# Four more units of eight tiles and closer final layers in a graph network's edge pass

## The chip, the cores and the metric

The kernel runs on one core of a Trainium2 chip. Its engines run their own instruction streams and wait for each other by semaphores: PE (matrix products), DVE and ACT (vector and scalar work), POOL (here it issues the indirect gathers), SP (here it issues plain transfers). The metric is the time of one execution on the device in microseconds (us), lower is better.

## The reference

```python
h = x                                        # 6250 nodes x 128; 100000 edges, sorted by dst
e = concat([h[src], h[dst]], axis=1)
a_k = exp(relu(e @ W_att_k + b_att_k))       # k = 1, 2, 3
att_k = segment_sum(a_k, dst)
avg_a = (a1/att1[dst] + a2/att2[dst] + a3/att3[dst]) / 3
m = avg_a * relu(relu(relu(h[src] @ W_msg_1 + b1) @ W_msg_2 + b2) @ W_msg_3 + b3)
h_neigh = segment_sum(m, dst) / max(deg, 1)
y = relu(concat([h, h_neigh], 1) @ W_c1 + b_c1) @ W_c2 + b_c2
out = layernorm(x + y)                       # without scale and bias
```

## The kernel before

**Stages.** First the three message layers run over all nodes and leave a table of message rows in memory (to about 69 us). Then one loop runs over units of edges. A tile is 128 edges, a group two tiles (256 edges, 391 groups), a unit four tiles or, in a long unit, eight. The first 108 groups, whose targets are the 512 busiest nodes, are not gathered: they are counted into a matrix (the count stage, units 0 to 26, four groups in each), and this matrix is multiplied with the message table block by block (the hot stage, units 29 to 77, one block of 128 nodes in each). The other 283 groups are gathered, and the loop over units handles them, in order of their target: `LONG` = 22 long units first, then 98 of four tiles, 120 in all. In ten of the long units (3, 5, ... 21) half of the tiles have no gather: their messages are computed from rows of `x` loaded before ("early" tiles).

**One unit.** POOL gathers a tile's message rows with one indirect DMA (L1428) into a ring of 12 places of four tiles; a long unit takes two places, and a place is free again when PE has summed the unit that held it. PE makes the one-hot products of a unit two ahead (`edge_q`, L1567), DVE adds the logits (L2078, and L2084, which waits for the gathered rows), ACT takes the exponent (L1763), DVE makes the weights (`weights`, L2104 and L2109), PE sums messages and weights into the nodes' window (`add_edges`, L1615, L1621), and DVE adds each group's window to the accumulator (`add_sums`, L2128, one add for each group). The order is written out by hand: at each step of the loop each engine's program names what it does next, and waits hold it there.

**Final layers.** When all edges of a block of nodes are in, its final layers start: 14 pieces, number 0 to 9 of four blocks ("wide"). Piece c starts at unit `final_at[c]`, and its steps follow one in a unit: step 0, PE turns the sums (L959, in `add_edges`); step 1, twelve products (L971) for the three heads, into the same three banks for all pieces; DVE makes the scales (L1113 to L1118); step 2, ACT scales the first head (L1050) into `v_fin`, which there is once, and DVE adds the other two for two of the four blocks (L1133); step 3, DVE does so for the other two; step 4, PE multiplies `x` and adds `v_fin` (L979, L982); step 5, ACT's relu (L1058), PE's second product (L987), DVE adds a bias to `x` (L1179); step 6, DVE adds and takes the moments (L1189 to L1197); step 7, ACT and DVE make the standard deviation ("refine", L1202 to L1212); step 8, ACT normalizes (L1100) and SP stores. `FINAL_EVERY` says how many units lie between the starts of two pieces: three after an even one and three after an odd one, so that piece 0 to 9 start at 81, 84, ... 108. In a unit, a step 1 goes first, then the pieces in order. Four waits tie a piece to the one before it:

```python
# wide_pe, step 1 (L971): all of the piece before is scaled
pe.wait_ge(s_fv[0], all_scaled(c - 1))
# wide_pe, step 4 (L979): the piece before has been added (L1189)
pe.wait_ge(s_fy[0], FINAL_Y * (c - 1) + 1)
# wide_act, step 2 (L1050): v_fin of the piece before has been used (L982)
act.wait_ge(s_fr[0], c)
# wide_act, step 5 (L1058): hidden of the piece before has been used (L987)
act.wait_ge(s_f2[0], c)
```

**The left-edge check.** DVE looks whether an edge lies outside its group's window: four steps (`left`) at units 0, 17, 18, 19, then PE transposes the result (L1705) at step 20 into a bank that the counting uses too, and DVE reduces it (`another_pass`, L2063 and L2067) at the end of step 21. So that the bank is free for it, PE waits before the transpose until DVE has added the counts of group 80 (L1940, in step 21), and the product that uses the bank next (group 84, PE's step 21, L1641) waits for the end of `another_pass`. DVE adds counts and makes their one-hots (L1925) in each of the steps 0 to 27; ACT makes the other side (L1782). SP issues a load of the hot logits behind the check.

Of the kernel before, what the change touches and what calls it, by code (L numbers as in the profile page):

```python
# [32 lines left out]
P = 128  # L33
# [20 lines left out]
HOT_GROUPS = 108  # L54
HOT_WIDTHS = (6, 9, 10, 12)
PAIRS = 4
LONG = 22
KEPT = 4608
RING = 12
TWO, THREE = 2, 3  # L60
# [4 lines left out]
EARLY = 10  # L65
EARLY_FROM, EARLY_EVERY = 3, 2
# [29 lines left out]
def gnn_program(nc, x, x_t, src, dst, w_first, w_rest, b_rows, table, hot_table, near_table, q_table, early_table, ok_table, out,  # L96
                n_edges):
    f32, bf16, i32 = mybir.dt.float32, mybir.dt.bfloat16, mybir.dt.int32
    ALU, ACT, AX = mybir.AluOpType, mybir.ActivationFunctionType, mybir.AxisListType.X
# [11 lines left out]
    n_hot = HOT_GROUPS  # L111
# [8 lines left out]
    def width_of(g):  # L120

        if g < n_hot:
            return HOT_WIDTHS[g // CELL]
        share = min(1.0, (g // CELL + 1) * CELL / n_groups)
        mean = 2 * GROUP * n_nodes / n_edges * share
        return min(WIN, 4 * -(-int(mean + 12 * share + 2 + 3.99) // 4))

    def items_of(g):

        w = width_of(g)  # L130
        most = n_blocks if w * n_blocks <= 512 else -(-n_blocks // TWO)
        return [(a, min(a + most, n_blocks)) for a in range(0, n_blocks, most)]

    def items_to(g):

        return sum(len(items_of(h)) for h in range(g))
# [4 lines left out]
    def counted(step):  # L141

        return range(step * PAIRS, min((step + 1) * PAIRS, n_hot))
# [5 lines left out]
    SPLIT_FROM = min(g for g in range(n_hot) if len(items_of(g)) > 1)  # L149
    assert items_to(SPLIT_FROM) == SPLIT_FROM and SPLIT_FROM % PAIRS == 0  # L150
    HOT_AT = COUNT_STEPS
    hot_end = HOT_AT + n_blocks + 2
    long_from = (n_hot // (2 * pair) + 1) * 2 * pair
    long_end = long_from + (LONG - 1) * 2 * pair
    assert long_end < n_groups and CELL % (2 * pair) == 0
# [4 lines left out]
    early_units = [EARLY_FROM + EARLY_EVERY * k for k in range(EARLY)]  # L160
    assert all(len(first_order[n]) == 2 * pair for n in early_units) and early_units[-1] < LONG
    early_groups = [first_order[n][pair:] for n in early_units]
# [17 lines left out]
    with ctx:  # L180
        def sb(name, shape, dt=f32):
            return ctx.enter_context(nc.sbuf_tensor(name, shape, dt))

        def sem(name):
            return ctx.enter_context(nc.semaphore(name))
# [29 lines left out]
        ident = sb("ident", [P, P])  # L215
# [65 lines left out]
        def hot_comb(t):  # L281

            j = t % HOT_RING
            return combs[j % TWO][:, j // TWO, :]
# [31 lines left out]
        least = sb("least", [P, 1])  # L316
        least_all = sb("least_all", [1, 1])
# [20 lines left out]
        bank = [ctx.enter_context(nc.psum_tensor(f"bank{i}", [P, 512], f32)) for i in range(8)]  # L338
# [12 lines left out]
        early_h, early_x, EARLY_BANK = staged[2], staged[1], 3  # L351
# [343 lines left out]
        Q_BANKS, SUM_BANKS, EXP_BANK, SIDE_BANKS = (1, 3), (0, 2), 4, (5, 6, 7)  # L695
# [2 lines left out]
        assert len(HOT_BANKS) == HOT and (HEADS + 1) * P <= 512  # L698
        assert columns_most + UNIT * PARTS <= 512

        LEFT_STEPS, LEFT_PE, LEFT_END = (0, 17, 18, 19), 20, 21


        assert LEFT_END < HOT_AT - 4 and LEFT_PE * PAIRS < n_hot
        ONES_AT = max(LEFT_END, early_units[-1])
        assert ONES_AT < HOT_AT - 2
        COUNT_BANKS = SIDE_BANKS + (EXP_BANK,)
        FOUR = len(COUNT_BANKS)
        LEFT_FREE = (LEFT_PE + 1) * PAIRS - FOUR + 1
        LEFT_NEXT = (LEFT_PE + 1) * PAIRS  # L710
        assert LEFT_NEXT < SPLIT_FROM
        LEFT_BANK = COUNT_BANKS[LEFT_NEXT % FOUR]
        HOT_ADDED = 3
        BOUND_AT, POWER_AT, OK_AT = 1, 2, 10
        BOUND_STEPS, OK_STEPS = 3, 5
# [10 lines left out]
        rest = n_blocks - sum(sizes) - 1  # L726
        sizes += [rest - rest // 2, rest // 2, 1]
        finals = [(sum(sizes[:c]), nb) for c, nb in enumerate(sizes)]
        FINAL_EVERY, FINAL_STEPS = (3, 3), 8
        LAST, LAST_FROM = len(finals) - 1, 2  # L730
        A, B, C = LAST - 3, LAST - 2, LAST - 1
        assert finals[LAST][1] == 1 and finals[B][1] <= LAST_FROM and finals[C][1] <= LAST_FROM
# [65 lines left out]
        s_left = sem("s_left")  # L798
        s_least = sem("s_least")
# [22 lines left out]
        s_erow = sem("s_erow")  # L822
# [7 lines left out]
        s_cadd = sem("s_cadd")  # L830
# [431 lines left out]
        def edge_pass(first):  # L1262

            order = first_order if first else again_order
            n_units = len(order)
            places = [2 if first and i < LONG else 1 for i in range(n_units)]
            place = [sum(places[:i]) for i in range(n_units)]
# [9 lines left out]
            def groups_to(i):  # L1277

                return sum(len(u) for u in order[:i + 1])
# [4 lines left out]
            def width(i):  # L1284
                return width_of(order[i][0])

            n_long = sum(n > 1 for n in places)
            assert all(n > 1 for n in places[:n_long])

# [17 lines left out]
            def early_turn(i):  # L1307

                return i // EARLY_EVERY if first and i < EARLY_EVERY * (EARLY + 1) else None
# [103 lines left out]
            with Straight(nc) if first else nc.Block() as block:  # L1413
# [127 lines left out]
                def _(pe):  # L1541
# [44 lines left out]
                    def first_early(k):  # L1586

                        pe.wait_ge(s_ecopy, k + 1)
                        pe.matmul(bank[EARLY_BANK][:, 0:COLS], w1, early_x, start=True, stop=True).then_inc(s_e1, 1)

                    def second_early(k):

                        pe.wait_ge(s_eh1, k + 1)
                        pe.matmul(bank[EARLY_BANK][:, 0:COLS], w2, early_h, start=True, stop=True).then_inc(s_e2, 1)
# [33 lines left out]
                    def count_edges(step):  # L1628

                        for g in counted(step):  # L1630
                            pe.wait_ge(s_lo, g // TWO + 1)
                            for j, (begin, end) in enumerate(items_of(g)):
                                item, w = items_to(g) + j, width_of(g)
                                if item >= FOUR:
                                    pe.wait_ge(s_cadd, item - FOUR + 1)
                                if item == LEFT_NEXT:
                                    pe.wait_ge(s_left, len(LEFT_STEPS) + 1)
                                for h in range(TILES):
                                    t = g * TILES + h
                                    pe.wait_ge(s_oh, t + 1)  # L1640
                                    pe.matmul(bank[COUNT_BANKS[item % FOUR]][:, 0:(end - begin) * w],  # L1641
                                              hot_lo[:, t % HOT_RING, :], hot_comb(t)[:, begin * w:end * w],
                                              start=h == 0, stop=h == TILES - 1).then_inc(s_ct, 1)
# [41 lines left out]
                    for i in range(n_steps):  # L1685
                        k = early_turn(i)
                        if i < n_units:
                            add_edges(i)
                        if k is not None and i % EARLY_EVERY == 1 and k < EARLY:
                            second_early(k)  # L1690
                        if first and i < COUNT_STEPS:
                            count_edges(i)
                        if k is not None and i % EARLY_EVERY == 0 and k < EARLY:
                            turn_early(k)
                        if i + 2 < n_units:
                            edge_q(i + 2)
                        if k is not None and i % EARLY_EVERY == 0 and k < EARLY:
                            first_early(k)
                        if k is not None and i % EARLY_EVERY == 1 and k < EARLY:
                            third_early(k)  # L1700
                        if i == LEFT_PE:
                            pe.wait_ge(s_left, len(LEFT_STEPS))
                            if first:
                                pe.wait_ge(s_cadd, LEFT_FREE)
                            pe.transpose(bank[LEFT_BANK][0:1, 0:P], least[:, :], ident[:, :]).then_inc(s_least, 1)  # L1705
                        if first and 0 <= i - HOT_AT - 2 < n_blocks:
                            hot_edges(i - HOT_AT - 2)
                        if first and i == hot_end:
                            turn_hot()
                        for c, step in final_steps(i):  # L1710
                            final_pe(pe, c, step, groups_to(ready[c]))
# [158 lines left out]
                def _(dve):  # L1870
# [189 lines left out]
                    def another_pass():  # L2060

                        dve.wait_ge(s_least, 1)
                        dve.tensor_reduce(least_all[:, :], bank[LEFT_BANK][0:1, 0:P], AX,  # L2063
                                          ALU.min).then_inc(s_left, 1)
                        dve.wait_ge(s_left, len(LEFT_STEPS) + 1)
                        if first:
                            dve.scalar_tensor_tensor(more[:, :], least_all[:, :], DONE, late[:, :],  # L2067
                                                     ALU.is_lt, ALU.max).then_inc(s_left, 1)
                        else:
                            dve.tensor_scalar(more[:, :], least_all[:, :], DONE, None, ALU.is_lt).then_inc(s_left, 1)  # L2070
# [65 lines left out]
                    for i in range(n_steps):  # L2136
# [40 lines left out]
                        if i == LEFT_END:  # L2177
                            another_pass()
# [119 lines left out]
```

## Time and profile before

| | |
|---|---|
| median of 3 runs | 774.49 us (770.85 to 776.41) |
| profiled execution | 772.04 us, of which the span of instructions is 767.9 us |
| mean granted clock of PE | 0.864 of full speed |
| busy: PE, DVE, POOL, ACT | 85%, 77%, 72%, 63% of the span |

A row of the timeline gives the start in us from the start of the span, the length of the row in us, engine, line, operation, names, the number of instructions that it merges, and in brackets the idle time before it with what ended it. Matmuls of 32-bit data stand as two records each.

### The profile page before, as it was taken

The page shows a single profiled execution, that of the slowest core. Times are in us where ns is not written, and L with a number is a line of the kernel's source. Part 1 is how long each engine was busy: PE and PEld are TensorE (multiplying, and loading weights), DVE is VectorE, ACT ScalarE, POOL GpSimd, SP SyncE. Part 2 cuts the span into 40 slices and gives each one's busy share as a digit, 9 for nine tenths or more (in the row PEclk, how much of TensorE's full clock was granted, in tenths as well). Part 3 has the DMA queues.
Part 4 walks back from the last instruction along what each step waited for, and adds up shares of the span by engine and source line. Part 5 has one row for each costly group of instructions (what it writes and reads, how often), then busy time and mean ns, then how long its engine had stood idle before and what let it go on. Part 6 is the DMA issues. An engine that isn't in the chain of part 4 may idle for free.

```text
span 767.9 us, 17623 instructions
## 1 busy us (share of the span) xinstructions
PE 651.9 (85%) x5388; PEld 535.7 (70%) x5388; DVE 593.9 (77%) x1881; ACT 486.6 (63%) x1128; POOL 553.2 (72%) x576
## 2 busy tenths in 40 slices
PE   8962679898879957789999999999988888888785
PEld 5752457765656633469999999999977777777664
DVE  4883577989777969877888888888765778777776
ACT  5554776877665536557777777777565555655563
POOL 7677777777777775467777777777777777777760
PEclk9985597879797776659999999999989788989797
DMA  7984353433883323223333333333352444445431
GB/s 224 258 207 105 67 80 82 97 81 79 77 71 86 67 59 88 46 56 72 82 79 81 79 81 80 82 82 79 76 137 65 107 131 107 118 105 136 101 95 34
DMA packets 81572, 73.70 MB, mean 96 GB/s; under 512 B 34056, under 2 KB 65472, under 8 KB 81472
## 3 DMA queue, kind: packets, MB, share of 16 engines
q0 software_dynamic: 18112, 37.94, 25.3%
q1 hardware_dynamic: 63072, 34.43, 16.8%
q8 instruction: 46, 0.75, 0.4%
q14 instruction: 54, 0.44, 0.2%
q10 hardware_dynamic: 288, 0.13, 0.1%
HBM read 62.91 MB, written 9.52 MB: 94 GB/s over the span
## 4 chain that ended last, share of the span: by engine, by line
PE 43%; POOL 22%; DVE 13%; issue 12%; ACT 6%; DMA 2%; DVEq 1%; SPq 0%; ACTq 0%
POOL work L1428 22%; PE bank L1660 15%; PE bank L1615 9%; PE bank L1641 3%; PE bank L1621 3%; DVE counts L1940 3%; DVE acc L1925 2%; DVE acc L2128 2%; ACT acc L1777 2%; PE bank L646 2%; PE bank L667 2%; PE bank L1567 1%; DMA work<-message_table,src_t 1%; PE bank L655 1%; PE bank L1572 1%
## 5 line engine op out<-in xcount | busy, mean ns | idle before, releaser
L1428 POOL DMA_INDIRECT work<-message_table,src_t x526 | 511.8, 973 | 178.4 <-issue 155.9
L1615 PE MATMUL bank<-work 128*128 128x144 f32 (+7 forms) x1132 | 175.8, 310 | 24.0 <-DVE acc L2128 23.9
L1615 PEld LDWEIGHTS bank<-work 128*128 128x128 f32 x1132 | 163.6, 220 | 33.8 <-issue 19.3
L1803 ACT COPY work<-bank 128x192 f32<-128x192 f32 (+5 forms) x120 | 36.0, 300 | 183.1 <-DVE work L2078 181.0
L2128 DVE TENSOR_TENSOR acc<-acc,bank 128x192 f32 (+7 forms) x283 | 85.9, 303 | 27.0 <-issue 4.4
L1660 PE MATMUL bank<-shared,acc 128*128 128x129 f32 (+1 forms) x784 | 95.6, 275 | 0.0
L2109 DVE TENSOR_TENSOR work<-bank,work 128x576 f32<-128x576 f32 (+5 forms) x120 | 83.5, 696 | 12.5
L1660 PEld LDWEIGHTS bank<-shared,acc 128*128 128x128 f32 (+1 forms) x784 | 91.5, 192 | 0.0
L1641 PE MATMUL bank<-acc 128*128 128x294 bf16 (+3 forms) x240 | 64.4, 406 | 29.6 <-ACT acc L1782 20.9
L1940 DVE TENSOR_TENSOR counts<-counts,bank 128x294 f32 (+3 forms) x120 | 68.9, 574 | 11.4 <-issue 7.5
L1641 PEld LDWEIGHTS bank<-acc 128*128 128x128 bf16 x240 | 23.1, 113 | 69.5 <-ACT acc L1782 36.5
L1984 DVE SCALAR_TENSOR_TENSOR acc<-logits_or_x,per_node,counts 128x512 f32<-128x512 f32 (+1 forms) x98 | 69.4, 749 | 0.0
L1755 ACT ACTIVATE side<-side,one_col 48x512 bf16<-48x512 bf16 (+1 forms) x93 | 66.9, 720 | 3.0
L1777 ACT ACTIVATE acc<-acc 128x128 bf16<-128x128 f16 x216 | 68.2, 386 | 0.0
L1753 ACT ACTIVATE side<-side,less_col 48x512 bf16<-48x512 bf16 (+1 forms) x93 | 65.7, 707 | 0.0
L1925 DVE TENSOR_SCALAR acc<-acc 128x294 bf16<-128x294 f16 (+3 forms) x216 | 65.3, 348 | 0.0
L1621 PE MATMUL bank<-work 128*4 128x48 f32 (+7 forms) x1132 | 63.0, 205 | 0.0
L1567 PE MATMUL bank<-side 48*128 48x57 bf16 (+7 forms) x566 | 35.7, 186 | 25.4 <-DMA side<-logit_parts 19.7
L1660 PE MATMUL bank<-work,acc 128*128 128x129 f32 (+1 forms) x392 | 56.7, 288 | 0.0
L1621 PEld LDWEIGHTS bank<-work 128*4 128x4 f32 x1132 | 44.6, 90 | 15.4 <-issue 3.1
L1567 PEld LDWEIGHTS bank<-side 48*128 48x128 bf16 x566 | 22.7, 96 | 42.0 <-issue 33.1
L1660 PEld LDWEIGHTS bank<-work,acc 128*128 128x128 f32 (+1 forms) x392 | 47.5, 191 | 2.2 <-issue 0.2
(188 smaller groups left out, 999.6 us busy)
## 6 DMA issues: line engine op xcount, KB each, us to landing
work<-message_table,src_t POOLq DMA_INDIRECT x526
side<-near_nodes SPq DMA_DIRECT2D x97, 48.0 KB
side<-logit_parts SPq DMA_DIRECT2D x283, 0.8 KB
message_table<-work SPq DMA_DIRECT2D x12, 262.0 KB, 4.5
work<-message_table SPq DMA_DIRECT2D x48, 65.5 KB, 1.8
work<-in_x_t SPq DMA_DIRECT2D x12, 256.0 KB, 4.2
counts<-in_x SPq DMA_DIRECT2D x11, 256.0 KB, 3.4
logits_or_x<-in_x_t SPq DMA_DIRECT2D x11, 256.0 KB
```

The source lines that it names most:

```text
L1428: pool.indirect_dma_start(out=rows_of(n)[:, t, :], out_offset=None, in_=table[:, :], in_offset=bass.IndirectOffsetOnAxis(ap=src_t[:, h, g: ...
L1615: pe.matmul(sums[:, at:at + HEADS * w], rows_here[:, t, 0:P], wt_of(i)[:, t, :], start=h == 0, stop=h == TILES - 1)
L1621: last = pe.matmul(sums[SUMS_AT:SUMS_AT + HEADS + 1, at + HEADS * w:at + HEADS * w + w], a_col[:, i % THREE, t, :], mask_of(i)[:, t, :], s ...
L1641: pe.matmul(bank[COUNT_BANKS[item % FOUR]][:, 0:(end - begin) * w], hot_lo[:, t % HOT_RING, :], hot_comb(t)[:, begin * w:end * w], start=h ...
L1660: last = pe.matmul(bank[HOT_BANKS[h]][:, k * (P + 1):(k + 1) * (P + 1)], hot_wt[0:m, b % THREE, k, h * P:(h + 1) * P], rows_here, start=Fa ...
L1755: act.activation(here, here, ACT.Relu, bias=one_col[0:WIN, 0:1], scale=-1.0).then_inc(s_hot, 1)
L1777: act.activation(hot_lo[:, t % HOT_RING, :], iota16[:, 0:P], ACT.Abs, bias=lo_t[:, g, h:h + 1], scale=-1.0).then_inc(s_lod, 1)
L1925: dve.tensor_scalar(hot_comb(t)[:, 0:n], iota16[:, 0:n], comb_t[:, g, h:h + 1], None, ALU.is_equal).then_inc(s_oh, 1)
L1940: dve.tensor_tensor(here, here, bank[COUNT_BANKS[item % FOUR]][:, 0:w * (end - begin)].rearrange("p (b d) -> p b d", d=w), ALU.add).then_i ...
L1984: dve.scalar_tensor_tensor(hot_wt[0:m, b % THREE, k, :], hot_b[0:m, k, :], inverse[0:m, b, k:k + 1], counts[0:m, b, :], ALU.max, ALU.mult) ...
L2109: dve.tensor_tensor(wt_of(i).rearrange("p t (k w) -> p t k w", w=w), from_q(i)[:, :, PARTS:PARTS + w].unsqueeze(2).to_broadcast([P, n, HEA ...
L2128: dve.tensor_tensor(here, here, sums[:, at:at + (HEADS + 1) * w].rearrange("p (k w) -> p k w", w=w), ALU.add).then_inc(s_acc, 1)
```

## The change

`LONG` goes from 22 to 26, so that units 22 to 25 take eight tiles each and every later unit begins eight groups further on; there are 116 units, four less. None of the four has early tiles. Piece starts are three and two units apart in turn: 81, 83, 86, 88, 91, 93, 96, 98, 101, 103, then 107 and 111 for the next two (before: 111 and 115). The check's transpose is at step 21, into bank 3, which only the early tiles use before the hot stage; the waits that tied it to the counting's bank are gone, and it waits for the last early tiles instead. `another_pass` is at the end of step 22. In the changed program lines behind L707 stand four or five lower numbers.

```diff
-LONG = 22
+LONG = 26
...
-        LEFT_STEPS, LEFT_PE, LEFT_END = (0, 17, 18, 19), 20, 21
...
-        assert LEFT_END < HOT_AT - 4 and LEFT_PE * PAIRS < n_hot
+        LEFT_STEPS, LEFT_PE, LEFT_END = (0, 17, 18, 19), 21, 22
...
+        assert LEFT_END < HOT_AT - 4 and EARLY_EVERY * EARLY < LEFT_PE
...
-        LEFT_FREE = (LEFT_PE + 1) * PAIRS - FOUR + 1
-        LEFT_NEXT = (LEFT_PE + 1) * PAIRS
-        assert LEFT_NEXT < SPLIT_FROM
-        LEFT_BANK = COUNT_BANKS[LEFT_NEXT % FOUR]
...
-        FINAL_EVERY, FINAL_STEPS = (3, 3), 8
+        FINAL_EVERY, FINAL_STEPS = (3, 2), 8
...
+            left_bank = EARLY_BANK if first else SIDE_BANKS[0]
...
-                                if item == LEFT_NEXT:
-                                    pe.wait_ge(s_left, len(LEFT_STEPS) + 1)
...
                         if i == LEFT_PE:
                             pe.wait_ge(s_left, len(LEFT_STEPS))
                             if first:
-                                pe.wait_ge(s_cadd, LEFT_FREE)
-                            pe.transpose(bank[LEFT_BANK][0:1, 0:P], least[:, :], ident[:, :]).then_inc(s_least, 1)
+                                pe.wait_ge(s_erow, EARLY)
+                            pe.transpose(bank[left_bank][0:1, 0:P], least[:, :], ident[:, :]).then_inc(s_least, 1)
```

Where the two waits of the check stand on PE, before (steps 20 and 21; `least` is the check's result, `s_cadd` counts DVE's adds of counts, `s_left` the check's steps):

```order
L1567 MATMUL bank<-side 128x41 [waits s_wt,s_eq,s_qw2]
L1567 MATMUL bank<-side 128x41 x3
L1705 MATMUL bank<-ident,least 1x128 [waits s_cadd,s_left]
L1615 MATMUL bank<-work 128x96 [waits s_acc,s_emsg,s_wt]
L1615 MATMUL bank<-work 128x96 x7
L1621 MATMUL bank<-work 4x32 x8
L1641 MATMUL bank<-acc 128x490 [waits s_left,s_oh,s_cadd,s_lo]
```

The same place on PE in the changed program (steps 21 and 22; `s_erow` counts the early tiles' rows):

```order
L1564 MATMUL bank<-side 128x41 [waits s_wt,s_eq,s_qw3]
L1564 MATMUL bank<-side 128x41 x7
L1700 MATMUL bank<-ident,least 1x128 [waits s_erow,s_left]
L1612 MATMUL bank<-work 128x96 [waits s_acc,s_wt]
L1612 MATMUL bank<-work 128x96 x7
L1618 MATMUL bank<-work 4x32 x8
L1636 MATMUL bank<-acc 128x490 [waits s_oh,s_cadd,s_lo]
```

The transpose no longer waits for DVE's counts, the counting no longer for the check, and the unit behind it has eight tiles (x7 and x8 there are a long unit's).

PE in the final layers before, one piece's step 1 (`s_fv` counts DVE's scaled blocks) and what follows it, in every piece:

```order
L971 MATMUL bank<-rest_w,acc 128x128 [waits s_fv0]
L971 MATMUL bank<-rest_w,acc 128x128 x11
L979 MATMUL bank<-logits_or_x,rest_w 128x512 [waits s_xg0,s_fy0]
L982 MATMUL bank<-ident,counts 128x128 [waits s_fv0]
L982 MATMUL bank<-ident,counts 128x128 x3
L1615 MATMUL bank<-work 128x144 [waits s_acc,s_wt]
L1615 MATMUL bank<-work 128x144 x3
L1621 MATMUL bank<-work 4x48 x4
L1567 MATMUL bank<-side 128x57 [waits s_wt,s_hot,s_qw0]
```

The same on PE in the changed program, for a piece that starts two units behind the one before it (pieces 1, 3, 5, 7 and 9):

```order
L967 MATMUL bank<-rest_w,acc 128x128 [waits s_fv0]
L967 MATMUL bank<-rest_w,acc 128x128 x11
L1612 MATMUL bank<-work 128x144 [waits s_acc,s_wt]
L1612 MATMUL bank<-work 128x144 x3
L1618 MATMUL bank<-work 4x48 x4
L1564 MATMUL bank<-side 128x57 [waits s_wt,s_hot,s_qw2]
L1564 MATMUL bank<-side 128x57 x3
L975 MATMUL bank<-logits_or_x,rest_w 128x512 [waits s_xg0,s_fy0]
L978 MATMUL bank<-ident,counts 128x128 [waits s_fv0]
L978 MATMUL bank<-ident,counts 128x128 x3
```

There a unit's sums and one-hot products now lie between the twelve products of one piece and step 4 of the piece before it; for the other pieces the order is as it was.

## Rows read from the trace of the kernel before

**Rows 1.** Stretches: length, busy us (instructions) by engine, granted clock, DMA share, GB/s.

```profile
565.00:747.00 182.00, 149.83 (x1263) 130.55 (x1262) 136.67 (x508) 107.03 (x270) 137.13 (x144) 0.88 0.43 106
...
643.70:650.50 6.80, 5.94 (x35) 5.63 (x32) 5.45 (x26) 3.18 (x10) 4.97 (x7) 0.50 0.51 143
...
661.00:668.00 7.00, 6.33 (x54) 5.50 (x54) 5.16 (x20) 4.47 (x13) 5.48 (x6) 1.00 0.46 117
...
717.00:722.00 5.00, 1.11 (x14) 0.83 (x12) 4.55 (x19) 1.20 (x3) 3.78 (x5) 0.50 0.44 102
```

**Rows 2.** The chain that ended last, 595 to 747 us, by line.

```profile
by line: POOL work L1428 48.4%; issue 21.7%; DMA work<-message_table,src_t 2.4%; DVE stats L1193 2.3%; DVE acc L2128 2.1%; ACT counts L1100 2.0%; DVE counts L1189 1.8%; DVE counts L1172 1.5%; DVE counts L1133 1.5%; PE bank L1615 1.5%; ACT c
```

**Rows 3.** POOL's waits, 227 to 350 us: total, times, longest (us).

```profile
POOL work L1428 <- PE bank L1621: 19.4, 7, 4.2
```

**Rows 4.** Timeline of DVE, count stage.

```profile
269.97 0.96 DVE L2109 TENSOR_TENSOR work<-bank,work 128x768 f32<-128x768 f32 x1
...
285.77 0.20 DVE L2078 TENSOR_REDUCE work<-bank 128x12 f32<-128x36 f32 x1 [3.58 <-PE bank L1567]
...
292.64 1.55 DVE L2128 TENSOR_TENSOR acc<-acc,bank 128x128 f32 x4 [0.49 <-issue]
...
299.43 0.56 DVE L2109 TENSOR_TENSOR work<-bank,work 128x384 f32<-128x384 f32 x1
299.91 0.33 DVE L2036 TENSOR_SCALAR side<-side,less_col 48x512 bf16<-48x512 bf16 x1
300.17 0.69 DVE L2128 TENSOR_TENSOR acc<-acc,bank 128x128 f32 x2
```

**Rows 5.** Timeline of PE, count stage.

```profile
274.93 0.37 PE L1705 MATMUL bank<-ident,least 128*1 128x128 f32 x1 [3.60 <-DVE counts L1940]
...
282.25 3.28 PE L1641 MATMUL bank<-acc 128*128 128x490 bf16 x8 [3.03 <-DVE more L2067]
```

**Rows 6.** Timeline of DVE, final layers.

```profile
644.00 1.22 DVE L1133 SCALAR_TENSOR_TENSOR counts<-bank,scale,counts 128x128 f32<-128x128 f32 x4
...
646.39 0.76 DVE L2109 TENSOR_TENSOR work<-bank,work 128x576 f32<-128x576 f32 x1
...
648.48 0.16 DVE L1202 TENSOR_TENSOR refine<-spread 128x4 f32<-128x4 f32 x1
...
649.40 0.19 DVE L2078 TENSOR_REDUCE work<-bank 128x12 f32<-128x36 f32 x1
...
650.42 0.76 DVE L2109 TENSOR_TENSOR work<-bank,work 128x576 f32<-128x576 f32 x1
651.10 0.83 DVE L2128 TENSOR_TENSOR acc<-acc,bank 128x192 f32 x2
651.85 0.68 DVE L1179 TENSOR_TENSOR counts<-counts,row_b 128x512 f32<-128x512 f32 x1
653.72 1.25 DVE L1133 SCALAR_TENSOR_TENSOR counts<-bank,scale,counts 128x128 f32<-128x128 f32 x4 [1.19 <-ACT counts L1050]
```

**Rows 7.** Timeline of PE, final layers.

```profile
645.28 5.42 PE L971 MATMUL bank<-rest_w,acc 128*128 128x128 f32 x24 [0.86 <-DVE counts L1133]
650.53 1.02 PE L979 MATMUL bank<-logits_or_x,rest_w 128*128 128x512 f32 x2
...
652.28 1.15 PE L1615 MATMUL bank<-work 128*128 128x144 f32 x8
...
654.00 1.16 PE L987 MATMUL bank<-rest_w,counts 128*128 128x128 f32 x8
...
661.02 2.94 PE L971 MATMUL bank<-rest_w,acc 128*128 128x128 f32 x24 [1.10 <-DVE counts L1133]
```

**Rows 8.** Timeline of ACT, final layers.

```profile
653.07 1.14 ACT L1050 ACTIVATE counts<-bank,scale 128x128 f32<-128x128 f32 x4
```

**Rows 9.** Waits, 565 to 747 us: total, times, longest (us).

```profile
DVE counts L1133 <- ACT counts L1050: 5.6, 8, 1.3
DVE work L2084 <- DMA work<-message_table,src_t: 5.4, 7, 2.5
```

More of the change, by code:

```diff
@@ L2062, in another_pass @@
                         dve.wait_ge(s_least, 1)
-                        dve.tensor_reduce(least_all[:, :], bank[LEFT_BANK][0:1, 0:P], AX,
+                        dve.tensor_reduce(least_all[:, :], bank[left_bank][0:1, 0:P], AX,
                                           ALU.min).then_inc(s_left, 1)
```

## The prediction

> **What bounds the kernel now.** I read the stretches first, then the chain, then the waits, then single units in the timeline.
>
> In the final layers, 565 to 747 us, PE is busy 149.8 of 182 us, DVE 136.7, POOL 137.1 [rows 1]: no engine is full, so the order decides. The chain names the gathers: 48.4% on POOL's line and 21.7% "issue", the gap between two gathers [rows 2]. POOL does run without a pause there. But whether it sets the pace is told by who waits for it: in the whole stretch DVE waits for gathered rows 7 times, 5.4 us in all, and 5.6 us, in 8 waits, for ACT's scaling of the first head [rows 9]. So the gathers are only just ahead, and DVE has hardly a wait of its own. One unit without a final step costs it 1.02 (L2078 to L2109) + 0.68 (L2109) + 0.75 (L2128 until the next) = 2.45 us [rows 6], and the final steps are added to that. DVE and POOL are close to a tie there, at about 5 us a unit (182 us for 36 units).
>
> POOL loses time earlier. Between 227 and 350 us it waits 7 times, 19.4 us in all, for PE's sums to give ring places back [rows 3]: units 22 to 31 take only four tiles each while counting makes them long.
>
> In the count stage DVE is the slower side too, and the check costs it directly: PE waits 3.60 us before the transpose and 3.03 us for the check's end, and DVE then stands 3.58 us until PE has made the next one-hot product [rows 4, 5].
>
> **The check's transpose.** In its new place it follows PE's sums of unit 21, which need the weights of unit 21; DVE makes these in step 20 behind the last early rows, so the new wait is over when it is reached. The 3.58 us on DVE go. On SP the load of the hot logits is issued one step later; behind it are one-hot inputs of units some steps ahead, and its reader is step 27. I put that at nothing: cover is the three units between, and without it a late load would show as a wait of unit 26's one-hots. Sum: -3.6.
>
> **Four long units in the count stage.** Each adds to DVE: weights 0.96 instead of 0.56, four adds of 1.55 instead of two of 0.69, one more one-hot of 0.33 [rows 4]: 0.40 + 0.86 + 0.33 = 1.6 us, four times 6.4. PE has its products doubled as well; they stand beside DVE's work as long as PE's idle time lasts. Nothing in the trace shows a long unit without early tiles beside counting. From below I take DVE's 6.4. From above: sums and one-hots of four tiles take PE 1.72 us in the final layers at the full clock [rows 7], 3.4 at the half, and two thirds of that, 2.3, with windows of 32 instead of 48 columns (128x128 and 128x192 in L2128's rows [rows 4, 6]); half of four times 2.3, 4.6 us, might come behind DVE's work instead of beside it. I take the lower end, since DVE had almost no idle time there but for the check. The stage becomes 6.4 - 3.6 = 2.8 us longer (to 7.4).
>
> **Fewer units behind.** Four units less at 2.45 us of DVE [rows 6]: -9.8. Since the long units give ring places back earlier, most of POOL's 19.4 us of waiting [rows 3] goes. That is no gain by itself: it counts only through DVE's 5.4 us of waiting for rows [rows 9], of which I take off 5.
>
> **Pieces two units apart.** This is the term that decides. Take piece 2 (starts at 86) and piece 3 (at 88). The twelve products of piece 3 (step 1, unit 89) wait until DVE has scaled the last block of piece 2, and that is step 3 of piece 2, in unit 89 as well, the last thing that DVE does there. Today these stand in two units one behind the other, and still PE just waits for it: 0.86 and 1.10 us before L971 [rows 7]. Then ACT may scale piece 3's first head only when `v_fin` of piece 2 has been used, in step 4 of piece 2: today that is on PE directly behind the twelve products, for piece 3 it is one unit later, behind the sums and one-hot products of unit 90. DVE is to go on with piece 3 in that same unit 90.
>
> Count from the end of DVE's scaling (t0). On PE: twelve products 5.25 us (645.28 to 650.53, granted clock 0.50, the lower level, 1.2 GHz) or 2.94 (661.02, granted clock 1.00, 2.4 GHz) [rows 1, 7]; the unit's sums and one-hots 1.72 (652.28 to 654.00); step 4 1.75 (650.53 to 652.28) [rows 7]; ACT for two of four blocks 0.57, half of 1.14 [rows 8]; start of PE 0.06. Sum 9.35 or 7.04. DVE itself needs 2.45 for the unit and 0.92 for the refine step of piece 1 (648.48 to 649.40) [rows 6], 3.37 together. It stands 6.0 us at the lower clock or 3.7 at the higher one. As a test of this way of counting: today's order at the lower clock gives 5.25 + 1.75 + relu and scaling on ACT behind it, and DVE was released 8.5 us after t0 (645.22 to 653.72), 1.19 us late [rows 6].
>
> It happens for pieces 1, 3, 5, 7 and 9: five times. Pieces with an even number start three units behind and have today's order. Which clock? PE stands before the twelve products while DVE does sums of scales, moments and a scaling in one unit; by the same rows, set behind each other, that is some 4 to 6 us (an estimate from rows 6 and 7). Where PE waited long for DVE now, 717 to 722 us with 1.11 us of work, the granted clock was 0.50 [rows 1]. I take the lower level four times, the higher once: 4 x 6.0 + 3.7 = 27.7. Bounds 18.5 and 30.0. Today's 5.6 us of such waits fall away, but for the one of the next narrow piece: -5.
>
> The Trainium skill, page "TensorE: Matmul & The Clock Gate", section "What's actually happening", says that the throttled state is the default and that activity releases it. By that all five waits would end at the lower level and the time would be 2.3 us higher; the trace has waits of 1.10 us after which the clock was still full [rows 1, 7], so it does not follow for every wait.
>
> **Sum.** Count stage +2.8; units -9.8; rows -5; today's scaling waits -5; new ones +27.7: together +10.7 us. Against the profiled execution, 772.04 (span 767.9 and 4.1 around it), 782.7. The median of the runs, 774.49, is 2.45 above that execution, and a median is what is asked, so 785.2; I write 785.
>
> **The rivals.**
>
> *The gathers set the pace and DVE's new waits are small (faster).* If DVE's new waits sum to under some 3 us, because ACT or PE reach the scaling earlier than I think, the terms are 2.8 - 9.8 - 5 - 5 + 3 = -14, and POOL, whose waiting falls by 19.4 less 0.3 for each of seven gathers, ends its last gather 17 us earlier, with the tail behind it unchanged: 757 to 760. For it: the chain's 48.4% [rows 2], and POOL busy in the same share of every stretch [rows 1]. Against it: the four waits in the program are explicit, and today's order already lets PE wait for DVE. It decides in five places, units 85, 90, 95, 100, 105. Chance 0.17.
>
> *Waits at the full clock.* 18.5 instead of 27.7: +1.5 us, 776. For it: the two waits before L971 that ended at full clock [rows 7]. Against it: longer idle time before. Chance 0.22.
>
> *Count stage on PE and all five at the lower clock.* 7.4 instead of 2.8 and 30.0 instead of 27.7: +6.9 on the forecast, 792. For it: PE at half clock in much of the count stage; against it, its idle time there. Chance 0.13.
>
> *The change does not do what it says.* The order shows 116 units and the moved wait, so I leave nothing for that but 0.03 of other mishaps on either side, such as transfers that collide.
>
> **How the numbers follow.** Forecast 785 with 0.45 (780 to 789 within it). Rival one lies at 758 (0.17), two at 776 (0.22), three at 792 (0.13). The range leaves out most of rival one and what lies above three: 766 to 794. About 1% is what a measurement of this kernel can tell from no change, so 766.7 and 782.2 are the marks. Faster: 0.17. Same: rival two, 0.22, and some of the forecast's lower side, together 0.29. Slower: 0.54.
>
> **What the changed profile would show.** In the list of waits, DVE's scaling (now L1129) waiting for ACT's (now L1046) some 28 us in all, with five waits of 3.5 to 6 us at units 85, 90, 95, 100 and 105; under 5 us in all would prove rival one's premise. The granted clock in these units tells forecast from rival two. POOL's wait for PE's sums before the hot stage falls from 19.4 to under 4 us. No wait of DVE for PE at the check (L2073), none of PE at L1700; units 22 to 25 about 1.6 us longer than short ones. DVE's wait for gathered rows under 1 us in the final layers. What would make the number wrong: PE reaching step 4 earlier than I count, a clock that stays full, or gathers that fall behind because of the units that are now shorter in the tail.

## The result and the profile after

The changed kernel takes 786.59 us (median of 4 runs, 781.70 to 790.94), the kernel before 773.40 in the same session: a ratio of 1.0167, 95% interval 1.0096 to 1.0239, so slower by about 12.9 us. The profiled execution took 786.47 us, its span is 782.6 (before 767.9), the mean granted clock 0.873 (before 0.864).

Where the time went is read first by stretches. The start of a unit's weights on DVE marks the stages; in the changed kernel these are the weights of unit 21, of unit 29 (the hot stage) and of unit 81 (the final layers), here in its timeline of DVE:

```profile
271.05 0.96 DVE L2104 TENSOR_TENSOR work<-bank,work 128x768 f32<-128x768 f32 x1
...
338.74 0.56 DVE L2104 TENSOR_TENSOR work<-bank,work 128x384 f32<-128x384 f32 x1
...
570.00 0.76 DVE L2104 TENSOR_TENSOR work<-bank,work 128x576 f32<-128x576 f32 x1
```

In the kernel before the same three rows start at 269.97 [rows 4] and here:

```profile
333.44 0.56 DVE L2109 TENSOR_TENSOR work<-bank,work 128x384 f32<-128x384 f32 x1
...
564.72 0.71 DVE L2109 TENSOR_TENSOR work<-bank,work 128x528 f32<-128x528 f32 x1
```

So:

| us | unit 21 to 29 | hot stage, 29 to 81 | 81 to the end |
|---|---|---|---|
| before | 63.5 | 231.3 | 203.2 |
| after | 67.7 | 231.3 | 212.6 |
| difference | +4.2 | 0.0 | +9.4 |

The start of unit 21 differs by 1.1 us, and nothing ahead of it was changed. (Among all the traces of this study it lies between 262.0 and 274.1, so stages have to be compared by their length and not by where they stand in the span.)

**The final layers.** The waits of 565 to 762 us in the changed kernel (engine and line, what it waited for, total us, times, longest):

```profile
ACT counts L1046 <- PE bank L978: 36.2, 5, 7.9
DVE counts L1129 <- ACT counts L1046: 29.4, 6, 6.4
PE bank L967 <- DVE counts L1129: 24.2, 5, 6.6
```

The middle row is the one that stood at 5.6 us in 8 waits [rows 9]. No wait of DVE for gathered rows is left (5.4 us before, [rows 9]). The six waits one by one, in the timeline of DVE:

```profile
582.50 1.25 DVE L1129 SCALAR_TENSOR_TENSOR counts<-bank,scale,counts 128x128 f32<-128x128 f32 x4 [1.31 <-ACT counts L1046]
595.64 1.25 DVE L1129 SCALAR_TENSOR_TENSOR counts<-bank,scale,counts 128x128 f32<-128x128 f32 x4 [4.91 <-ACT counts L1046]
628.73 1.25 DVE L1129 SCALAR_TENSOR_TENSOR counts<-bank,scale,counts 128x128 f32<-128x128 f32 x4 [6.41 <-ACT counts L1046]
659.88 1.25 DVE L1129 SCALAR_TENSOR_TENSOR counts<-bank,scale,counts 128x128 f32<-128x128 f32 x4 [5.55 <-ACT counts L1046]
693.73 1.25 DVE L1129 SCALAR_TENSOR_TENSOR counts<-bank,scale,counts 128x128 f32<-128x128 f32 x4 [6.18 <-ACT counts L1046]
724.91 1.25 DVE L1129 SCALAR_TENSOR_TENSOR counts<-bank,scale,counts 128x128 f32<-128x128 f32 x4 [5.07 <-ACT counts L1046]
```

Five of them are new, one for each odd piece, 28.1 us in all. What leads to one is seen in PE's timeline around the third row, with ACT's row behind it:

```profile
619.02 5.36 PE L967 MATMUL bank<-rest_w,acc 128*128 128x128 f32 x24 [6.59 <-DVE counts L1129]
624.21 1.15 PE L1612 MATMUL bank<-work 128*128 128x144 f32 x8
...
625.93 1.12 PE L975 MATMUL bank<-logits_or_x,rest_w 128*128 128x512 f32 x2
626.89 1.05 PE L978 MATMUL bank<-ident,counts 128*128 128x128 f32 x8
```

```profile
628.07 1.14 ACT L1046 ACTIVATE counts<-bank,scale 128x128 f32<-128x128 f32 x4 [7.92 <-PE bank L978]
```

PE stands 6.59 us until DVE has scaled the even piece, makes the twelve products of the odd piece (5.36 us where the full clock takes 2.94 [rows 7]), then the unit's sums and one-hots, and only then uses `v_fin` (L978). ACT may overwrite it after that, and DVE goes on 0.66 us after ACT has begun (628.07 to 628.73). The windows of these stretches show the granted clock (length, busy us and number of instructions of PE, PEld, DVE, ACT, POOL, then granted clock, DMA share, GB/s):

```profile
612.00:619.00 7.00, 0.42 (x9) 0.22 (x6) 5.23 (x21) 3.01 (x7) 5.36 (x6) 0.88 0.54 141
619.00:624.10 5.10, 5.08 (x24) 5.08 (x25) 2.56 (x11) 1.02 (x4) 3.78 (x4) 0.50 0.40 107
```

PE does 0.42 us of work in 7, and the twelve products behind that run at 0.50. Of the five sets of products of odd pieces four are slow (5.36, 4.57, 5.22 and 4.57 us); over the two of 4.57 us the mean granted clock is 0.63, so a part of each ran at the full clock. The first set, after a wait of 2.75 us, ran wholly at the full clock:

```profile
588.35 2.94 PE L967 MATMUL bank<-rest_w,acc 128*128 128x128 f32 x24 [2.75 <-DVE counts L1129]
...
650.95 4.57 PE L967 MATMUL bank<-rest_w,acc 128*128 128x128 f32 x24 [4.33 <-DVE counts L1129]
```

**POOL.** Its waits for ring places, 227 to 350 us, were 19.4 us [rows 3] and are now

```profile
POOL work L1425 <- PE bank L1618: 0.9, 3, 0.3
```

and the last gather ends at 727.4 us instead of 745.9. POOL is done 18.5 us earlier, and the kernel ends later. In the chain of work that ended last (part 4 of the profile's page, shares by engine), first before and then after the change, POOL had 22% and now has none:

```profile
PE 43%; POOL 22%; DVE 13%; issue 12%; ACT 6%; DMA 2%; DVEq 1%; SPq 0%; ACTq 0%
...
PE 56%; DVE 20%; ACT 10%; issue 7%; DMA 4%; DVEq 2%; SPq 1%; ACTq 0%; POOLq 0%
```

**The check.** PE's transpose and DVE's first sums of one-hot products (L2073) behind it have no wait any more (3.60 and 3.58 us in [rows 4, 5]):

```profile
282.15 0.27 PE L1700 MATMUL bank<-ident,least 128*1 128x128 f32 x1
```

```profile
283.59 0.23 DVE L2073 TENSOR_REDUCE work<-bank 128x24 f32<-128x72 f32 x1
...
292.28 0.27 DVE L2058 TENSOR_REDUCE least_all<-bank 1x1 f32<-1x128 f32 x1
...
292.68 0.21 DVE L2073 TENSOR_REDUCE work<-bank 128x24 f32<-128x72 f32 x1
```

### The profile page after: what moved, and what is told of

Same layout as the page of the kernel before. It is cut to its first block, busy times and chain, and to the rows that moved or that the text cites. A ratio compares the mean times of both kernels' runs of the same rounds, so it can differ in the third digit from the quotient of the medians.

```text
span 782.6 us, 17558 instructions
## 1 busy us (share of the span) xinstructions
PE 648.6 (83%) x5388; PEld 536.3 (69%) x5388; DVE 593.8 (76%) x1869; ACT 479.6 (61%) x1112; POOL 550.2 (70%) x576
## 4 chain that ended last, share of the span: by engine, by line
PE 56%; DVE 20%; ACT 10%; issue 7%; DMA 4%; DVEq 2%; SPq 1%; ACTq 0%; POOLq 0%
PE bank L1655 18%; PE bank L1612 11%; PE bank L967 4%; PE bank L1618 4%; DVE counts L1935 3%; DVE acc L2123 3%; PE bank L1636 3%; DVE acc L1920 2%; PE bank L1564 2%; ACT acc L1772 2%; PE bank L646 2%; PE bank L667 2%; DMA shared<-early_rows 2%; DVE counts L1129 1%; ACT counts L1829 1%
## 5 line engine op out<-in xcount | busy, mean ns | idle before, releaser
L1798 ACT COPY work<-bank 128x192 f32<-128x192 f32 (+6 forms) x116 | 35.3, 304 | 172.9 <-DVE work L2073 172.8
L2104 DVE TENSOR_TENSOR work<-bank,work 128x576 f32<-128x576 f32 (+6 forms) x116 | 82.9, 715 | 12.1
L1636 PE MATMUL bank<-acc 128*128 128x294 bf16 (+3 forms) x240 | 59.6, 378 | 25.9 <-ACT acc L1777 19.6
L1920 DVE TENSOR_SCALAR acc<-acc 128x294 bf16<-128x294 f16 (+3 forms) x216 | 67.2, 355 | 0.0
L1750 ACT ACTIVATE side<-side,one_col 48x512 bf16<-48x512 bf16 (+1 forms) x89 | 64.0, 720 | 2.9
L1636 PEld LDWEIGHTS bank<-acc 128*128 128x128 bf16 x240 | 22.5, 109 | 62.8 <-ACT acc L1777 29.4
L1748 ACT ACTIVATE side<-side,less_col 48x512 bf16<-48x512 bf16 (+1 forms) x89 | 62.9, 707 | 0.0
L1564 PE MATMUL bank<-side 48*128 48x57 bf16 (+7 forms) x566 | 34.8, 186 | 33.7 <-DMA side<-logit_parts 20.3
L967 PE MATMUL bank<-rest_w,acc 128*128 128x128 f32 x240 | 39.4, 338 | 24.2 <-DVE counts L1129 24.2
## 6 DMA issues: line engine op xcount, KB each, us to landing
message_table<-work SPq DMA_DIRECT2D x12, 262.0 KB, 4.4
```

Of the source, the lines that this page charges most:

```text
L967: last = pe.matmul(packed(i, k), acc[:, k, (b + i) * P:(b + i + 1) * P], wc1[:, 1, :], start=True, stop=True)
L1564: last = pe.matmul(from_q(i)[:, t, :], near_of(i)[:, t * P:(t + 1) * P], q_eye[:, slot(i, t // TILES), 0:PARTS + width(i)], start=t == 0 i ...
L1920: dve.tensor_scalar(hot_comb(t)[:, 0:n], iota16[:, 0:n], comb_t[:, g, h:h + 1], None, ALU.is_equal).then_inc(s_oh, 1)
L2104: dve.tensor_tensor(wt_of(i).rearrange("p t (k w) -> p t k w", w=w), from_q(i)[:, :, PARTS:PARTS + w].unsqueeze(2).to_broadcast([P, n, HEA ...
```

## The experiments

The theory: the slowdown is the five waits in the final layers, made by the two-unit spacing through one buffer, `v_fin`; the check and the long units gain, but less. The rivals: the slowdown sits in the count stage (long units), or in the clock alone, or in gathers that come late (no wait of DVE for rows, above, speaks against that). Ratios are against the kernel before on the same chip; microseconds from a ratio are worked out on 773.4. The changed kernel's own ratio, 1.0167, is known to about 0.7% (5.5 us) either way, and every difference to it below carries that; the waits and stretches come from one trace of each kernel.

### The check alone

The changed kernel with the long units and the spacing of before:

```diff
-LONG = 26
+LONG = 22
...
-        FINAL_EVERY, FINAL_STEPS = (3, 2), 8
+        FINAL_EVERY, FINAL_STEPS = (3, 3), 8
```

> Of the change only the check's transpose one step later in bank 3; 22 long units and pieces three units apart as before. Theory (DVE stood 3.58 us behind the check, on the path): 3 to 4 us less than before, about 770, and no wait of DVE for PE behind the check in the profile. Rival (the stall is given back later, since the gathers pace the final layers): within 1 us of before.

Measured: 768.34 us, ratio 0.9949 (0.9925 to 0.9973), -3.9 us. Units 21 to 29 take 59.5 us instead of 63.5, the other two parts are as before (230.8 and 203.1). The moved transpose is a gain of its own, and of the size of the one wait that it takes from DVE.

### The spacing alone

The kernel before with this edit only:

```diff
-        FINAL_EVERY, FINAL_STEPS = (3, 3), 8
+        FINAL_EVERY, FINAL_STEPS = (3, 2), 8
```

> Of the change only the pieces three and two units apart; 22 long units and the check as before. Theory (five waits of DVE for the first head's scaling, 28 us in all, less today's 5.6 us of such waits and 5 us of waits for gathered rows): about 17 us more than before, 790. Rival (the gathers set the pace): POOL is untouched here, so within 3 us of before, 773. If the eight-tile units were what costs: no change either.

Measured: 791.85 us, ratio 1.0278 (1.0238 to 1.0319), +21.5 us where about 17 were expected; from unit 81 to the end 225.7 us instead of 203.2. The 17 took off 5 us of waits for gathered rows, of which 2.8 are still there, and counted 28 us of new waits, of which there are 29.5 (all five sets of odd products slow, 4.57 to 5.49 us). Its wait of DVE for ACT's scaling, 565 to 762 us, has the size of the one in the changed kernel:

```profile
DVE counts L1133 <- ACT counts L1050: 30.1, 6, 6.9
```

One number in the list of spacings makes all of the loss and more; the count stage as its cause is out. The long units alone were not run: in 116 units the first narrow piece starts at 107, and ten wide pieces three units apart would have the last at 108. Their share is read from pairs of kernels, below.

### A second buffer for the first head

The changed kernel with two buffers in place of `v_fin`, used in turn by the pieces; ACT waits for the piece before the last. PE (L978) and DVE (L1129) take the same one of the two:

```diff
+        v_at = 6 * COLS + n_out
+        v_wide = [v_fin, fin[:, v_at:v_at + COLS].rearrange("p (i f) -> p i f", f=P)]
...
-                if c >= 1:
-                    act.wait_ge(s_fr[0], c)
+                if c >= 2:
+                    act.wait_ge(s_fr[0], c - 1)
...
-                    act.activation(v_fin[:, i, :], packed(i, 0), ACT.Copy,
+                    act.activation(v_wide[two][:, i, :], packed(i, 0), ACT.Copy,
...
```

> The changed kernel with a second buffer for the scaled heads of the wide pieces, so that ACT need not wait for the piece before to be used. Theory: the five waits of DVE (28 us in all) shrink by the 3.5 us that PE spends on the unit's sums and on step 4, to some 9 to 11 us; time 17 to 19 us less than the changed kernel's 786.6, about 768. Rival (PE's twelve products and the clock are the cost, not the buffer): waits shrink by under 5 us, 782 or more.

Measured: 771.52 us, ratio 0.9986 (0.9967 to 1.0006), 14.0 us less than the changed kernel. The wait falls by 15.1 us:

```profile
DVE counts L1131 <- ACT counts L1048: 14.3, 6, 2.9
```

So the buffer was half of the five waits; what is left of each, up to 2.9 us, is the twelve products, which still start late and still run mostly at the lower level. I had expected about 768, with waits of 9 to 11 us. The sum behind it, 28 less five times 3.5, leaves the products as they are in the changed kernel, one set of them at the full clock; all five sets are slow here, even the one before which PE waits as briefly as in the changed kernel (2.76 and 2.75 us):

```profile
589.27 4.57 PE L969 MATMUL bank<-rest_w,acc 128*128 128x128 f32 x24 [2.76 <-DVE counts L1131]
...
618.06 5.49 PE L969 MATMUL bank<-rest_w,acc 128*128 128x128 f32 x24 [6.65 <-DVE counts L1131]
```

### Step 4 directly behind the twelve products

The same aim with one buffer: PE does step 4 of the even piece directly behind step 1 of the odd one, one unit earlier than in the changed kernel, in the order that all pieces had before. `close` holds the odd pieces.

```diff
                         for c, step in final_steps(i):
+                            if step == 4 and c + 1 in close:
+                                continue
                             final_pe(pe, c, step, groups_to(ready[c]))
+                            if step == 1 and c in close:
+                                final_pe(pe, c - 1, 4, groups_to(ready[c - 1]))
```

> The changed kernel with step 4 of an even piece directly behind the twelve products of the odd piece, ahead of the next unit's sums; one buffer as before. Theory: only the unit's sums and one-hots (1.7 us) leave the chain, five times: 8 to 9 us less than 786.6, about 778. Rival (the wait is for the products alone): no change, 785 to 788.

Measured: 779.17 us, ratio 1.0069 (1.0040 to 1.0099), 7.6 us less than the changed kernel; the wait is 20.1 us, 9.3 less. The five crossings of a unit's sums (1.72 us each at the full clock [rows 7]) are worth 8.6, so near enough the step that was taken out. The time's interval only just touches that of the changed kernel (1.0096 to 1.0239).

### DVE's scaling ahead of the older piece

DVE does step 3 of an even piece before the moments of the piece ahead of it, so that PE may begin the twelve products earlier:

```diff
-                        for c, step in final_steps(i):
+                        for c, step in sorted(final_steps(i), key=lambda e: e[1] != 3 or e[0] + 1 not in close):
                             final_dve(dve, c, step)
```

> The changed kernel with DVE's two final steps swapped in the units that decide: the last scaling of the even piece stands before the adds and moments of the piece before it, so that PE's twelve products start 1.9 us earlier while DVE does the moments. Theory: each of the five waits shrinks by 1.9 us: 9 to 10 us less than the changed kernel's 786.6, about 777. Rival (the moments are waited for as well, so the time comes back): within 3 us of 786.6.

Measured: 774.64 us, ratio 1.0031 (1.0003 to 1.0060), 10.5 us less than the changed kernel; the wait is 20.3 us in 5, 9.1 less. Nothing was changed but the order of two pieces of DVE's work: the odd piece was late because PE's start hung on the last thing that DVE did in a unit. Not each wait shrank by the 1.9 us expected: the last four fell by 2.0 to 3.6 us, while the first rose from 4.91 to 7.33, its products taking 5.49 us here and 2.94 in the changed kernel. So a part of what each wait gained or lost is the clock's, and not the order's.

### PE kept busy

Ahead of each odd piece's step 1, ten products of the unit matrix with itself go into columns of a bank that nobody reads, once those are free. They add work on PE (and one wait of their own) and leave the rest of the order as it is; only the clock of what follows can gain. `FILL` is 10.

```diff
+                            if step == 1 and c in close:
+                                pe.wait_ge(s_acc, groups_to(i - 1))
+                                for _ in range(FILL):
+                                    pe.matmul(bank[SUM_BANKS[(i + 1) % TWO]][:, 3 * P:TURNED], ident[:, :], ident[:, 0:TURNED - 3 * P],
+                                              start=True, stop=True)
                             final_pe(pe, c, step, groups_to(ready[c]))
```

> The changed kernel with ten products of no use (128x128 times 112 columns, results unread) on PE ahead of the wait for the last scaling, in the five places: about 2.2 us at the full clock, 4.4 at half, in a wait of 3 to 7 us. Theory (the lower clock after the wait is part of the price): the twelve products take 2.9 us in all five places instead of 4.6 to 5.4 in four, and the time falls by 5 to 9 us, to 778 to 782. Rival (the order alone is the price, or the clock falls all the same): products as slow as before, 785 to 790, or later if the filling itself delays them.

Measured: 777.71 us, ratio 1.0093 (1.0062 to 1.0123), 5.7 us less than the changed kernel with more work, though the two intervals overlap; in the traces the wait is 23.4 us, 6.0 less. PE's timeline at one odd piece:

```profile
643.24 2.48 PE L1711 MATMUL bank<-ident 128*128 128x112 f32 x20 [1.52 <-DVE acc L2130]
...
646.30 2.94 PE L968 MATMUL bank<-rest_w,acc 128*128 128x128 f32 x24 [0.58 <-DVE counts L1130]
```

and DVE's wait behind it:

```profile
653.60 1.25 DVE L1130 SCALAR_TENSOR_TENSOR counts<-bank,scale,counts 128x128 f32<-128x128 f32 x4 [3.90 <-ACT counts L1047]
```

The twelve products are back at 2.94 us and the wait is 3.90, where 3.7 was worked out for the full clock. So the lower clock is a part of the loss and can be told from the order: 1.7 to 2.3 us in each of the last four waits (4.56, 3.90, 3.90 and 3.42 us instead of 6.41, 5.55, 6.18 and 5.07). The Trainium skill, page "TensorE: Matmul & The Clock Gate", section "What's actually happening", has the throttled state as the default, which activity releases; this run agrees with that (2.94 us behind the filling), while the 2.94 us behind 2.75 us of waiting in the changed kernel shows that not each wait brings that state back. At the first odd piece the filling itself came late (it ended 2 us after DVE's scaling, and took 3.42 us), and the wait there was 6.90 instead of 4.91: at that place the filling cost 2 us.

### Both mends, and both with 22 long units

Second buffer and DVE's scaling first, together on the changed kernel; and the same with `LONG = 22`:

> The changed kernel with the second buffer for scaled heads and the scaling before the moments. Theory: the waits that the second buffer left (14.3 us, 2.9 each) shrink by 1.9 each to about 1: 9 us less than the 771.5 of the second buffer alone, about 762, under the kernel before by some 1.3%. Rival (the gathers then set the pace): their last one ends at 730 with long units, which with the tail of 22 us behind it gives no less than 752, so they would not show; if they did, 768 or more.

> As the run with both mends, but with 22 long units (120 units in all). Theory: 16 tiles go back from the count stage (6.4 us less of DVE there) to four units more (9.8 us of DVE), and the last gather ends at about 741 instead of 730, with a tail of 22 us or more behind it: 763 to 768, so 2 to 5 us more than with 26. Rival (long units cost more than they bring): less than with 26.

Measured: 760.00 us, ratio 0.9841 (0.9801 to 0.9880), and 764.21 us, 0.9895 (0.9846 to 0.9943). Both are faster than both kernels of the case. The waits of the first, 565 to 742 us, and of the second, 565 to 744:

```profile
DVE counts L1131 <- ACT counts L1048: 4.4, 5, 1.3
```

```profile
DVE work L2082 <- DMA work<-message_table,src_t: 6.4, 6, 1.7
...
DVE counts L1131 <- ACT counts L1048: 4.7, 2, 3.2
```

The five long waits are gone in the first; in the second one of 3.2 us is left, at the first odd piece. With 22 long units DVE then waits for gathered rows (6.4 us); with 26 it does not in this trace. So the gathers can matter once the final layers stand close without waiting.

Over the kernels that mend the final layers, the time gained on the changed kernel goes with the wait taken from DVE:

| changed kernel with | wait of DVE for ACT's scaling, us | less wait | unit 81 to the end, us | less stretch | less time (from ratios) |
|---|---|---|---|---|---|
| nothing | 29.4 | | 212.6 | | |
| PE kept busy | 23.4 | 6.0 | 209.6 | 3.0 | 5.7 |
| scaling first | 20.3 | 9.1 | 207.0 | 5.6 | 10.5 |
| step 4 early | 20.1 | 9.3 | 202.4 | 10.2 | 7.6 |
| second buffer | 14.3 | 15.1 | 198.4 | 14.2 | 14.0 |
| both mends | 4.4 | 25.0 | 186.0 | 26.6 | 25.2 |

In two traces the stretch shrank by clearly less than the wait. These two executions, of scaling first and of PE kept busy, came to unit 21 at 263.1 and 262.0 us, the other four of the table at 271.1 to 274.1; and in these two alone DVE waits for gathered rows again, with 26 long units too (565 to 762 us, in that order):

```profile
DVE work L2080 <- DMA work<-message_table,src_t: 4.4, 4, 3.3
...
DVE work L2086 <- DMA work<-message_table,src_t: 4.7, 4, 2.2
```

The gathers are thus only just ahead with 26 long units as well: in the two executions in which DVE came early, it was held by them.

## Why the prediction was right

It gave 785 for a time of 786.59. The sum of its terms was +10.7; +13.6 stands in the stretches (4.2 in the count stage for 2.8, 9.4 in the final layers for 7.9) and +12.9 in the ratio. That the time itself is only 1.6 us off is in part luck: the sum was put on 774.49, and the kernel before measured 773.40 in the end.

- **Spacing: new waits 27.7, old ones -5, so +22.7.** The five new waits are 28.1 us, and the spacing alone costs 21.5. Shown by its own run, and by three that each take away one link of the chain that was counted (buffer, order on PE, order on DVE). The single sizes: 6.0 was counted at the lower clock, and 6.41, 5.55, 6.18 and 5.07 were found; 3.7 at the full clock, and 4.91. The wait of 4.91 is that of the first odd piece, where no piece stands ahead whose refine step (0.92 us) DVE could do meanwhile; with filling, a later one came to 3.90. Of the old scaling waits 1.3 us are left; they belong to piece 0 (582.50) and not, as was said, to the next narrow piece.
- **One wait at the full clock and four at the lower.** So it is in the trace of the changed kernel (2.94 us once, 4.57 to 5.36 four times). Rival two, all five at the full clock, is out: the run that kept PE busy shows what it would have needed. That it would fall on 1 of 5 was a choice, not worked out, and that it came true is luck: with the second buffer and with the spacing alone it was 0 of 5. Rival three (all five at the lower level, the count stage 7.4 longer) is out by the same rows: one set was at the full clock, and the stage is 4.2 us longer.
- **Units and gathered rows: -9.8 and -5.** In pairs of kernels that differ in the long units (the first pair in the check as well, which is over by then), unit 81 to the end falls from 225.7 to 212.6 (spacing alone against the changed kernel), by 13.1, and with both mends from 202.8 to 186.0, by 16.8; predicted 14.8.
- **Count stage: +6.4 for four long units, -3.6 for the check.** The check is -3.9. The long units cost more than I took: 67.7 us from unit 21 to 29 against 59.5 with the check alone, +8.2, and with both mends 67.7 against 59.6, the same. The term was mis-sized by 1.8 us, inside its bound of 11. The windows of this stretch, with the check alone and in the changed kernel, tell where:

```profile
269.60:329.14 59.54, 42.65 (x241) 24.85 (x241) 50.18 (x150) 33.09 (x87) 38.17 (x40) 0.67 0.28 69
...
271.05:338.74 67.69, 44.02 (x320) 29.78 (x321) 56.48 (x161) 33.63 (x87) 51.23 (x55) 0.76 0.32 78
```

DVE's own work (the third of the busy times) grew by 6.3 us, as counted (6.4); the other 1.8 us are idle time of DVE (9.4 and 11.2 us), which the sum did not have. DVE's waits for PE's counting products (L1636) are only 0.4 and 1.2 us of it, so of the 4.6 us that the upper bound put behind DVE for PE little shows.

- **Rival one, the gathers as the bound.** The last gather ended 18.5 us earlier (17 was said for that), and of that only the 5.4 us in which DVE had waited for rows were there to be gained. Its condition, hardly any new waits, is met only by the kernel with both mends (4.4 us of scaling waits in all, 5.6 before), and that one takes 760.00 (761.1 by its ratio on 773.4), where the rival was put at 757 to 760.
- **The four long units as a whole** come to -13.1 + 8.2 = -4.9 and -16.8 + 8.2 = -8.6 in the traces, and -4.2 by the medians of the last two kernels, whose intervals overlap: a small gain, not settled more closely.

## What to carry to other kernels

Before pieces of a pipelined stage are set closer, write down for every buffer that they share at which step it is filled and at which it is emptied, with the order on each engine: one unit less of spacing let the emptying of one piece fall behind other work, and five such places cost more than four units less gave. The chain of work that ended last named the gathers with 48.4%, yet ending them 18.5 us earlier took away no more than the 5.4 us that DVE had waited for them; who waits for an engine, and how long, told the bound better than its share of the chain. Where one engine waits at the end of another's unit, try the order of the independent steps on the other one first: a sort of one list was worth about 10 us here, and a second buffer about 14.

## What was not expected of the hardware

- The wait alone does not tell the clock that follows. After 2.75 and 2.76 us of waiting at the same place the twelve products took 2.94 us in the changed kernel and 4.57 with the second buffer. With DVE's scaling first, PE waited 2.57 us before two of the five sets, and they took 2.94 and 4.36 us. After waits of 4.3 to 6.7 us, in the changed kernel and with the second buffer, the products never ran wholly at the full clock.
- More work on PE made other work on it shorter: products that nobody reads (2.48 us in the row shown), ten in each of five places, brought the products behind them, which had taken 4.57 to 5.36 us, down to 2.86 to 2.94 in four of the five (in the fifth they rose from 2.94 to 3.59). The kernel went from 1.0167 to 1.0093; the intervals (1.0096 to 1.0239 and 1.0062 to 1.0123) overlap, so that the whole became faster is likely and not settled.
